# A key matmul over 512 context tokens instead of 256, in a float32 perceiver layer

## What is computed

```python
q = heads(layernorm(x), Wq, bq);  k = heads(ctx, Wk, bk);  v = heads(ctx, Wv, bv)   # HD = 32
q_prime, k_prime = relu(q @ Wqf.T), relu(k @ Wkf.T) * mask                          # 64 features a head
kv, k_sum = k_prime^T v, sum(k_prime)                    # summed over the 12,544 tokens
x = x + (q_prime kv / (q_prime k_sum + 1e-8)) @ Wo.T + bo
x = x + gated cumulative attention with w_qkv, w_swiglu, w_out     # w_swiglu: u and gate halves
x = x + top-1 of 2 experts with w_fc, w_proj
```

## Time and profile before

| | us |
|---|---|
| times of three executions | 925.14, 928.49, 929.46 |
| their median | 928.49 |
| span of the profiled execution, first to last instruction | 924.8 |
| PE busy | 907.2 |
| DVE, ACT, POOL busy | 646.5, 558.9, 356.4 |

### The profile page before, as it was taken

The page is one execution under the profiler, slowest core; times in us unless marked ns, Lnnn a source line. Parts: engine busy times, 40 slices in busy tenths (PEclk is TensorE's granted clock), DMA queues, the critical chain, the costliest instruction groups (busy, mean ns, idle before and its releaser), DMA issues.

```text
span 924.8 us, 16889 instructions
## 1 busy us (share of the span) xinstructions
PE 907.2 (98%) x5606; PEld 764.2 (83%) x5606; DVE 646.5 (70%) x1183; ACT 558.9 (60%) x1062; POOL 356.4 (39%) x163
## 2 busy tenths in 40 slices
PE   6999999999999999999999999999999998999998
PEld 4899999999999999999999999999999997444443
DVE  3777777777777777777777777777777776422422
ACT  3577777767777777777676777677777764100000
POOL 1345454545454545454544444454545442000000
PEclk8999999999999999999999999999999999999999
DMA  5121211212121211010101010101010103704800
GB/s 206 63 76 59 77 69 67 73 63 81 55 90 46 91 45 68 23 45 23 45 23 45 23 45 23 45 23 45 23 45 23 45 2 118 319 0 175 370 1 11
DMA packets 14460, 64.03 MB, mean 69 GB/s; under 512 B 2160, under 2 KB 3952, under 8 KB 13424
## 3 DMA queue, kind: packets, MB, share of 16 engines
q1 hardware_dynamic: 13440, 61.52, 18.1%
q10 hardware_dynamic: 1008, 2.35, 0.7%
HBM read 63.60 MB, written 0.26 MB: 69 GB/s over the span
## 4 chain that ended last, share of the span: by engine, by line
PE 90%; issue 6%; DVE 2%; DMA 1%; ACT 1%; POOL 0%; SPq 0%; POOLq 0%; DVEq 0%; ACTq 0%
PE k_bank L517 11%; PE k_bank L518 10%; PE k_bank L519 10%; PE kv_ps L570 10%; PE f_ps L560 10%; PE v_bank L517 10%; PE v_bank L518 10%; PE v_bank L519 9%; PE kv_ps L730 3%; PE v_bank L627 2%; PE k_bank L627 2%; DMA ctx_raw<-in_ctx 1%; PE k_bank L613 1%; DVE kf L836 0%; PE f_ps L618 0%
## 5 line engine op out<-in xcount | busy, mean ns | idle before, releaser
L320 POOL TENSOR_TENSOR ksum_acc<-ksum_acc,kf 128x1024 f32<-128x1024 f32 x97 | 233.4, 2406 | 289.3 <-DVE kf L831 285.4
L806 DVE SCALAR_TENSOR_TENSOR keys<-k_bank,bias_cols,keys 64x256 fp32r<-64x256 f32 x392 | 189.5, 483 | 91.0 <-ACT keys L384 86.7
L517 PE MATMUL k_bank<-ctx_hi,wk_lo 128*128 128x256 f32 x784 | 231.9, 296 | 5.9 <-POOL ctx_lo L336 5.0
L403 ACT ACTIVATE fb<-f_ps 128x256 f32<-128x256 f32 x392 | 150.0, 383 | 142.9 <-PE f_ps L560 132.8
L518 PE MATMUL k_bank<-ctx_lo,wk_hi 128*128 128x256 f32 x784 | 222.6, 284 | 0.0
L519 PE MATMUL k_bank<-ctx_hi,wk_hi 128*128 128x256 f32 x784 | 222.5, 284 | 0.0
L384 ACT ACTIVATE keys<-k_bank,bias_cols 64x256 fp32r<-64x256 f32 x392 | 184.0, 469 | 41.7 <-PE k_bank L519 38.0
L824 DVE TENSOR_TENSOR kf<-f_ps,fb 128x256 f32<-128x256 f32 x392 | 164.1, 419 | 59.0 <-ACT fb L403 55.8
L517 PEld LDWEIGHTS k_bank<-ctx_hi,wk_lo 128*128 128x128 f32 x784 | 150.5, 192 | 32.0 <-DVE keys L806 24.3
L313 POOL TENSOR_TENSOR ctx_lo<-ctx_raw,ctx_hi 128x1024 fp32r<-128x1024 f32 x48 | 115.7, 2410 | 119.2 <-ACT ctx_hi L376 119.2
L560 PE MATMUL f_ps<-bd,keys 128*128 128x256 f32 x784 | 157.1, 282 | 2.5 <-DVE kf L824 2.5
(11 more groups left out here) (151 smaller groups left out, 733.1 us busy)
## 6 DMA issues: line engine op xcount, KB each, us to landing
ctx_raw<-in_ctx SPq DMA_DIRECT2D x49, 512.0 KB, 3.3
early<-in_early SPq DMA_DIRECT2D x22, 512.0 KB, 4.3
w_out<-in_wout SPq DMA_DIRECT2D x1, 4096.0 KB, 14.2
fc<-in_fc SPq DMA_DIRECT2D x1, 4096.0 KB, 24.9
early<-in_proj SPq DMA_DIRECT2D x1, 4096.0 KB, 12.4
early<-in_fc SPq DMA_DIRECT2D x1, 4096.0 KB, 21.7
w_out<-in_proj SPq DMA_DIRECT2D x1, 4096.0 KB, 20.6
early<-in_wk SPq DMA_DIRECT2D x2, 512.0 KB, 8.9
```

Source lines behind the costliest of these rows:

```text
L320: pool.tensor_tensor(ksum_acc[:, :].rearrange("p (j f) -> p j f", f=P), ksum_acc[:, :].rearrange("p (j f) -> p j f", f=P), kf[:, t, :, :], ...
L403: act.activation(fb[:, i % 2, :, :], f_ps[i % 2][:, :].rearrange("p (j x f) -> p j x f", j=2, x=2) [:, :, 1, :], ACT.Copy).then_inc(fb_rea ...
L517: pe.matmul(out_ps, st_lo, mv_hi, start=start, stop=False, **kw)
L806: last = dve.scalar_tensor_tensor(out=keys_2[other, s, 2 * g + h, :], in0=k_bank[rows, (g % 2) * CHUNK:(g % 2 + 1) * CHUNK], scalar=bias_c ...
```

## The change

A chunk is 512 tokens, as two halves of 256 (`HALF`); `ctx_raw` still holds one half, and the walk of 49 halves becomes a first period of one half and 24 of 512 tokens (`LAST` is 24). A period has four tiles; in each, `keys` makes one block `m` for 512 tokens with 12 matmuls of 512 columns. The first period makes the keys of 512 tokens in two tiles, with two blocks each. `k_hi_ready` and `k_lo_ready` now count halves of partitions of a block. Half of the gate weights, `swi_b`, leaves `early` (14 pieces now) and is loaded after the walk, behind `w_o`; `proj0` is loaded after two gate steps, not four. Cut to its core:

```diff
-            def keys(c, s, b, first=False, beside=None):
-                pe.wait_ge(ctx_lo_ready, c + 1)
-                if not first:
-                    pe.wait_ge(k_lo_ready, 2 * c + b)
-                for m in (2 * b, 2 * b + 1):
-                    for k in range(KC):
-                        last = three(k_bank[:, (m % 2) * CHUNK:(m % 2 + 1) * CHUNK],
...
+            def keys(c, s, m, jobs=()):
+                pe.wait_ge(ctx_lo_ready, 2 * c + 1)
+                pe.wait_ge(k_lo_ready, 2 * (KC * c + m))
+                for k in range(KC):
+                    last = three(k_bank[:, :], wk_hi[:, k, m * P:(m + 1) * P], wk_lo[:, k, m * P:(m + 1) * P],
+                                 ctx_hi[:, s, k, :], ctx_lo[:, s, k, :], k == 0, k == KC - 1)
+                    if k == KC - 1:
+                        last.then_inc(k_done, 1)
+                    if k % 2 == 0 and jobs:
+                        feature_job(*jobs[k // 2])
...
+            def period_0():
+                for t in range(2):
+                    jobs = [(0, 0, t, t, i, True) for i in range(JOBS)]
+                    if t == 0:
+                        pe.wait_ge(k_lo_ready, 4)
+                    values(t, 0, 2 + t, t == 0, jobs[0:2])
+                    keys(1, 1, 2 * t, jobs[2:4])
+                    keys(1, 1, 2 * t + 1)
+                pe.wait_ge(qf_ready, 2)
+                key_values(0, 0, first=True)
+
+            def period(c, s, last=False):
+                n = 4 * c - 2
+                for t in range(TILES):
+                    jobs = [(c, s, n + t, t, i) for i in range(JOBS)]
+                    if last:
+                        values(n + t, s, t, False, jobs)
+                    else:
+                        values(n + t, s, t, False, jobs[0:2])
+                        keys(c + 1, 1 - s, t, jobs[2:4])
+                    key_values(n + t - 1, t + 1)
```

```diff
@@ gpsimd
-            def period(c, s, first=False, last=False, split=True):
-                add_features(TILES * c, 0, first)
-                if split:
-                    split_ctx_low(c + 2, s)
-                if not last:
-                    add_features(TILES * c + 1, 1)
+            def period(c, s, last=False, split=True):
+                n = 4 * c - 2
+                for t in range(TILES):
+                    if not (last and t == TILES - 1):
+                        add_features(n + t, t)
+                    if split and t % 2 == 1:
+                        split_ctx_low(2 * c + 3 + t // 2, s, t // 2)
...
+            split_ctx_low(1, 1, 0)
+            split_ctx_low(2, 1, 1)
+            add_features(0, 0, True)
+            split_ctx_low(3, 0, 0)
+            add_features(1, 1)
+            split_ctx_low(4, 0, 1)
@@ scalar
+            def tile(n, t, first=False, last=False, last_tile=False, keys=(), split=None):
+                features_share(n, 0, first and t == 0)
+                if not (first and t == 0):
+                    features_high(n - 1, t - 1)
+                features_share(n, 1, first and t == 0)
+                if last:
+                    features_share(n, 2, False)
+                    features_share(n, 3, False)
+                if last_tile:
+                    features_high(n, t)
+                values_high(n, t, first)
+                if split:
+                    split_ctx_high(*split)
+                if not last:
+                    features_share(n, 2, False)
+                    features_share(n, 3, False)
+                for k in keys:
+                    keys_high(*k, k_bank, CHUNK)
...
+            split_ctx_high(2, 1, 1)
+            tile(0, 0, first=True, keys=((1, 1, 0), (1, 1, 1)), split=(3, 0, 0))
+            tile(1, 1, first=True, keys=((1, 1, 2), (1, 1, 3)), split=(4, 0, 1))
@@ vector
+                features_sum(n, t, 0, first)
+                if not (first and t == 0):
+                    features_low(n - 1, t - 1)
+                features_sum(n, t, 1, False)
+                if not last:
+                    values_low(n, t)
+                for i in range(2, JOBS):
+                    features_sum(n, t, i, False)
+                masked_features(n, t)
+                if last_tile:
+                    features_low(n, t)
+                if last:
+                    values_low(n, t)
+                for k in keys:
+                    keys_low(*k, k_bank, CHUNK)
@@ sync
+            sp.dma_start(swi_b[:, :], swib_in).then_inc(swib_loaded, 16)
             sp.dma_start(w_out[:, :, :], wout_in).then_inc(wout_loaded, 16)
             sp.dma_start(fc0[:, :, :], fc_in[0, :, :, :]).then_inc(fc0_loaded, 16)
+            sp.wait_ge(u_done, 2)
+            sp.dma_start(proj0, proj_in[0, :, :, :]).then_inc(proj0_loaded, 16)
             sp.wait_ge(u_done, 4)
-            sp.dma_start(proj0, proj_in[0, :, :, :]).then_inc(proj0_loaded, 16)
```

More of the change, by code:

```diff
@@ L118, in perceiver_kernel @@
         w_qkv = early[:, QKV_AT:SWI_AT].rearrange("p (k n) -> p k n", k=KC)
[L119 to L122, removed]
+        swi_a = early[:, SWI_AT:EARLY]
+        w_swi = [x.rearrange("p (k n) -> p k n", k=KC) for x in (swi_a, swi_b[:, :])]
+        proj0 = swi_a.rearrange("p (k n) -> p k n", n=D)
+        fc1 = swi_b[:, :].rearrange("p (k n) -> p k n", k=KC)
         def staged(at, n):
@@ L348, in _ @@
             pool.wait_ge(rms_eps_set, 1)
-            period(NC - 1, 0, last=True, split=False)
+            period(LAST, 0, last=True, split=False)
             rstd(2, 8, 2)
@@ L372, in _, with split_ctx_high, keys_high @@
             act.dma_start(mask[:, :], mask_in).then_inc(mask_loaded, 16)
[L374 to L387, removed]
+            def split_ctx_high(h, s, half):
+                act.wait_ge(ctx_loaded, 16 * h + 16)
+                act.activation(ctx_hi[:, s, :, half * HALF:(half + 1) * HALF], ctx_raw[:, :, :], ACT.Copy)\
+                   .then_inc(ctx_hi_ready, 1)
+            def keys_high(c, s, m, src, n):
+                act.wait_ge(k_done, KC * c + m + 1)
+                for h in range(2):
+                    rows = slice(PAIR * h, PAIR * (h + 1))
+                    act.activation(keys_2[rows, s, 2 * m + h, 0:n], src[rows, 0:n], ACT.Identity,
+                                   bias=bias_cols[rows, KC + m:KC + m + 1]).then_inc(k_hi_ready, 1)
             def values_high(n, t, first):
@@ L439, in split_wk_high, with period @@
+            def period(c, s, last=False, split=True):
+                for t in range(TILES):
+                    tile(4 * c - 2 + t, t, last=last, last_tile=last and t == TILES - 1,
+                         keys=() if last else ((c + 1, 1 - s, t),),
+                         split=(2 * c + 3 + t // 2, s, t // 2) if split and t % 2 == 1 else None)
             def split_wk_high(b):
-                cols = slice(b * CHUNK, (b + 1) * CHUNK)
+                cols = slice(b * HALF, (b + 1) * HALF)
@@ L635, in _ @@
             pe.wait_ge(ctx0_lo_ready, 1)
-            keys(0, 0, 0, first=True)
+            pe.wait_ge(ctx_lo_ready, 1)
+            keys_0(0)
+            keys_0(1)
             pe.wait_ge(ident_loaded, 16)
@@ L647, in _ @@
             pe.wait_ge(wk_lo_ready, 2)
-            keys(0, 0, 1)
+            keys_0(2)
+            keys_0(3)
             pe.wait_ge(q_ready, 1)
@@ L657, in _ @@
             pe.wait_ge(wv_lo_ready, 1)
-            period(0, 0, first=True)
-            with pe.Fori(1, NC - 2, 2) as c:
+            period_0()
+            with pe.Fori(1, LAST - 1, 2) as c:
                 period(c, 1)
                 period(c + 1, 0)
-            period(NC - 2, 1)
-            period(NC - 1, 0, last=True)
+            period(LAST - 1, 1)
+            period(LAST, 0, last=True)
             pe.wait_ge(ksum_ready, 1)
@@ L876, in _ @@
             dve.wait_ge(bias_loaded, 32)
-            keys_low(0, 0, 0)
+            for m in range(2):
+                keys_low(0, 0, m, k_first[m], HALF)
             dve.wait_ge(q_done, 1)
@@ L885, in _ @@
                .then_inc(wv_lo_ready, 1)
-            keys_low(0, 0, 1)
+            for m in range(2, 4):
+                keys_low(0, 0, m, k_first[m], HALF)
             for b in range(2):
@@ L892, in _ @@
             dve.wait_ge(mask_loaded, 16)
-            period(0, 0, first=True)
-            with dve.Fori(1, NC - 2, 2) as c:
+            tile(0, 0, first=True, keys=((1, 1, 0), (1, 1, 1)))
+            tile(1, 1, first=True, keys=((1, 1, 2), (1, 1, 3)))
+            with dve.Fori(1, LAST - 1, 2) as c:
                 period(c, 1)
                 period(c + 1, 0)
-            period(NC - 2, 1)
-            period(NC - 1, 0, last=True)
+            period(LAST - 1, 1)
+            period(LAST, 0, last=True)
             dve.wait_ge(kv_done, NT)
```

234 lines of the change are left out of this document (98 added, 136 removed).

## The result

| | before | after |
|---|---|---|
| median of the runs, us | 926.82 (4 runs) | 1017.36 (4 runs, 1012.96 to 1019.07) |
| span of the profiled execution, us | 924.8 | 1015.0 |
| mean granted clock | 0.994 | 0.971 |

The change makes the kernel slower: ratio 1.098, 95% interval 1.096 to 1.101. The prediction said 1007, with 966 to 1028.

What follows compares the result with a forecast made beforehand. PE was taken as the bound. Walk terms 28.5 + 682.6 + 67.1 + 32.1 = 810.3 against 751.2 gave +59; with 20 for clock on 924.8, 1003.8, stated as 1007 for the median; range 966 to 1028.

Steps and rivals of the forecast that it cites:

- The forecast's case: In the walk, DVE and POOL take turns and half clock follows some of the stalls; time 1007, chance 0.43.
- Wider key matmuls, and the wait on `keys_low`: In each tile, 512-column key matmuls cost 3.23 instead of 3.36 and PE's 0.09 wait goes; a tile takes 7.42.
- POOL's order: In tile 0, POOL makes the low part after the features, so `keys` starts about 2.1 late; periods 2 to 23.
- DVE and POOL together: In tile 0, `features_low` and POOL's instructions take turns, lengthening the stall to 3.05, 22 times.
- DVE comes first, which is closer: In tile 0, `features_low` is ready at 2.64, against 2.77 for POOL's second instruction, and holds POOL up.
- POOL could get its second instruction in: Rival: POOL precedes DVE, stall 2.05, 23 tiles grow by 1.2, the same 59 to 61; chance 0.15.
- The first period: At the walk's start, key blocks wait for loads, splits and the emptied bank; 28.5 instead of 15.5.
- The last period: At the walk's end, four tiles without keys, three of 7.2 and 10.4 for the last and its tail; 32.1.
- Granted clock: After the 22 stalls, a drop to half clock costs 1.8; half of all was taken, 20.
- Loads: After the walk `swi_b` and in the loop `ctx_raw` load hidden behind other work; 0.

Runs made afterwards that it cites:

- low_first: The changed kernel, but in tiles 1 and 3 of a period POOL makes the low part before adding the features; 918.49 us, ratio 0.994.
- before_pool: The kernel before, but POOL adds the features of tile 1 ahead of the low part of the next chunk but one; 1021.23 us in one run.
- after_warm: The changed kernel, but PE makes nine useless 512-column matmuls before waiting for the low part in tile 0 of the loop's periods; 996.31 us, ratio 1.078.
- after_small_low: The changed kernel, but `features_low` of the odd tiles works on 128 of its 1024 columns; 991.58 us, ratio 1.072.

## Why the prediction came out as it did

The forecast's case held (the stall, the turns, half clock after some stalls), and 1007 was 10 too low: the span came out 11.2 above its sum of 1003.8, and the median of the runs lies 2.4 above that span where the forecast had added 3.7. By its own steps:

- **Wider key matmuls, and the wait on `keys_low`.** Right: 7.42 a tile in all 92 of low_first, each of the two parts to 0.01. Together they are worth 20 us in the loop, and two tiles fewer 15. The two ends take 30 of it back (31.5 + 31.8 against 15.5 + 17.7), which is why low_first gains only 0.6%.
- **POOL's order.** Right in place, cause and periods: 22 stalls from period 2 on, gone in low_first, and made in the kernel before by before_pool.
- **DVE and POOL together.** Right that they take turns, and right in size where DVE is first: 3.14 for 3.05. That DVE comes first each time was the step that failed. The forecast's "DVE comes first, which is closer" and its rival "POOL could get its second instruction in" were put as one or the other; what it had at 2.64 and 2.77 stands at 2.70 and 2.71 in the trace, and both orders happen, POOL first in 5 of 22 tiles 0 and in 13 tiles 2. The rival's price held (2.07 in tile 0, 1.17 in tile 2, for 2.05 and 1.2). Since a period can pay DVE's price in tile 0 and POOL's in tile 2, stalls and long tiles come to 78.8 where the sum had 67.1: the stalls are 3.5 under it, and tile 2, which the sum had at nothing, is 15.2. That is +11.7. By the measured prices DVE always first would have cost 22 x 3.14 = 69 and POOL always first 22 x 2.07 + 23 x 1.17 = 72; the mixture costs more than either. The rival's own sum was wrong too: 22 x 2.05 + 23 x 1.2 = 72.7 is 5.6 more than 67.1, so its walk was 65 longer, and not "the same 59 to 61".
- **The first period.** Block 2 waits 4.57 (4.8 forecast), block 4 waits 2.68 (2.8), but the period takes 31.5 for 28.5. The granted clock is 0.83 in its window: both waits are followed by half clock, and the step had counted that for the loop alone. From their first matmul to what comes next block 2 takes 4.98 and block 4 4.42, each 2.76 in the forecast: +3.9. The other way, block 1 waits only 0.27 for its low part where 1.5 were forecast, and block 2 starts 0.9 sooner. +3.0.
- **The last period.** 31.8 for 32.1.
- **Granted clock.** 12 of 22 stalls and 19.3 us in the loop, for "half of 22" and 20; after_warm gives the same 20. The price of one, 1.8 by the earlier trace rows, is 1.3 to 1.6 here, once 2.7.
- **Loads.** Nothing waits for `swi_b`, and in the loop nothing for `ctx_raw`; in the first period ACT waits for it 0.72 and 3.08, as that step had reckoned. The part after the walk is 143.0 in the changed kernel, as in low_first. Right.

Sum of the misses: 11.7 + 3.0 - 0.7 - 0.3 in the walk, less 2.7 outside it, is 11.0, and 1003.8 + 11.0 = 1014.8 is within 0.2 of the measured span of 1015.0.

The Trainium skill (SBUF — State Buffer, section "Who interferes with whom") makes the port pair that DVE and GpSimd share an exclusive lock, and has whoever issues first hold it for the whole instruction. The trace agrees in both directions: 3.42 for POOL behind DVE's 1.23, and 3.50 for DVE behind POOL's 2.41. One after the other the two take 3.64, so their spans overlap by 0.1 to 0.2.

**What stays open** is which stalls are followed by half clock. It isn't the longest: in the changed kernel 4 of the 5 waits of 1.8 were, and 8 of the 17 of 2.9; in after_small_low 15 of 22 waits of 1.81 to 1.96; in before_pool 4 of 47 of 1.7 to 1.8, with a stall every 17.2 us instead of every 32 to 36. No run here separates the length from the distance.

## What to carry to other kernels

When a loop is made longer, read anew for each engine what its last instruction of a turn is, and who waits for it at the head of the next: here two instructions of 2.4 us in the wrong order, on an engine that is 38% busy, cost 98 us, where the rest of the change gains 6. Where two engines reach a shared resource within hundredths of a microsecond, price both orders place by place: here both occurred in one execution, and the mixture cost more than either. And measure the parts of a change alone: half of this one's gain in the loop was a finer wait, and the old structure with that finer wait alone is 12 us faster than before.

## What the hardware showed that I had not expected

- The order of DVE and POOL at a near tie isn't fixed by the recorded starts: with DVE recorded 0.01 ahead both times, DVE went first at 400.94 and POOL at 418.93.
- A stall that draws half clock and one that doesn't can't be told by their length (above), and useless matmuls in 2.1 of a stall's 2.9 us took all half clock out of the loop.
